# The opening reordered: tile 3's shift in its own buffer, high Wo products ahead of low, rows of products that nobody reads in TensorE's pauses

## The chip, the cores and the metric

The kernel runs on one core of a Trainium2 chip. The metric is the device time of one launch in microseconds (us), and the median of several runs stands for a kernel. A core has five engines that work side by side, each through its own queue in order: TensorE (PE in the profile), VectorE (DVE), ScalarE (ACT), GpSimd (POOL), and SyncE (SP), which here issues the transfers. They meet at semaphores. A page of the profile comes from one profiled execution.

## The reference, cut to what matters

One layer on 2 x 2048 tokens of width 512. `x` is normalised, attends to 64 latent keys per head with the four largest logits, is added and normalised again, and goes through a feed-forward block whose three weight matrices are reduced to three values:

```python
Q = (hidden_states @ Wq.T + bq)...; V = (hidden_states @ Wv.T + bv)...
attn_logits = einsum('bhtd,lhd->bhtl', Q, latent) / sqrt(HD)        # 16 heads, 64 latents
topk_logits, topk_idx = top_k(attn_logits, 4)
weighted = einsum('bhtk,bhtkd->bhtd', softmax(topk_logits), selected)
attn_output = (weighted + V) @ Wo.T + bo

scale = mean(abs(w)) + 1e-8                                          # for W_up, W_gate, W_down
w = clip(round(w / scale), -1, 1) * scale
ffn = (silu(x @ wu.T) * (x @ wg.T)) @ wd.T

x = x + layernorm(attention(layernorm(x)))
x = x + layernorm(ffn(layernorm(x)))
```

## The kernel before

The 4096 tokens are eight chunks of 512, a chunk is four tiles of 128 tokens. Every float32 factor is split into a high and a low float16 half ("hi", "lo"); a product is two or three float16 products that add up in PSUM. The order on each engine is written out by hand, as a list of calls per body. There are five bodies: "first" (attention of chunk 0), "second" (attention of chunk 1 beside the feed-forward block of chunk 0), "mid" in a loop, "last" and "tail". Every body but "first" starts with the Q products of its chunk (`q`), then 16 column blocks of up and gate products (`upgate`), with the attention of the next chunk between them, then the down products.

The change lies in "first" and the head of "second". What happens there in the kernel before:

- **Selection of the four largest**, tile by tile: VectorE finds the maxima (`maxes`) and marks them (`replace`, into `Lr`), POOL subtracts the largest (`shift`, in place in `Lb`), ScalarE takes the exponential (`exps`), VectorE keeps the marked ones (`select`), POOL normalises (`normalise`, line 1242, into `p`), ScalarE and VectorE write the high and low halves (`probs_hi`, `probs_lo`), SyncE transposes both into `PT` (`pt`). `Lb` has two buffers, tile t in buffer t % 2.
- **Value products** (`weigh_half(0)` for tiles 0 and 1, `weigh_half(1)` for 2 and 3), evicted by ScalarE (`vw_half`) with the low half on POOL (`low_a_half`, line 1215).
- **Wo**: `wo_first(0)` gives the output of tiles 0 and 1, the products with the high weights first, then those with the low weights of Wo (from `weights_lo(2)` on VectorE). `wo(2)` and `wo(3)` give the rest. From each output VectorE and POOL make layer norm, residual and second layer norm (`y_a`, `rstd_y`, `y_b`, `rstd_x`, `y_c`), ScalarE and VectorE the rows' two halves (`t2_rows`, `t2_lo`, in `halves[t % 2]`), SyncE the transposed `X1T` (`t2`, line 377).
- **The next chunk's rows** go the same way to `XT` (`ln1_stat(1)`, `s1_rows`, `s1_lo`, `s1`). Their split lies in two buffers in `Lr`, so tile 2 waits for the transposition of tile 0.
- **The three-valued weights**: each matrix is loaded in eight pieces (0 to 7 up, 8 to 15 gate, 16 to 23 down) into memory that is used later for something else; pieces 0 and 8 lie in `X1T`. `abs_sum` adds absolute values per piece, `tern_total(w)` adds those of a matrix, a product with ones (`total`, line 537) adds over the partitions, `tern_scale_of(w)` makes the scale; `round_to(n)` on VectorE (line 1440) rounds a piece, `sign(n)` on ScalarE (line 882) writes the final one. The first transposition of `X1T` waits for signs 0 and 8.

TensorE's order in "first" ends with `wo(3)` and the gate's total, which waits for VectorE. "second" begins with `q(0)`, which waits for all of `XT`. `upgate(0)` and `upgate(1)` run in two halves of 256 tokens, then come the logits of tiles 0 and 1, then `upgate(2)`.

## Time and profile before

| | |
|---|---|
| median of 3 runs | 1037.1 us (1036.57 to 1037.91) |
| the profiled execution | 1038.45 us, its span 1036.7 us |
| mean granted TensorE clock | 0.981 |
| TensorE busy | 968.7 us, 93% of the span |
| VectorE, POOL, ScalarE busy | 731.3, 535.0 and 514.1 us |
| column block 2 of the feed-forward block starts | 121.67 us after the span's start |

The page has the busy share of each engine in 40 equal slices of about 26 us, in tenths. The timeline lists instructions with their start, their duration and, in brackets, the idle time before them with what ended it. All times count from the start of the span, which is 1.75 us shorter than the whole time of the profiled execution.

### The profile page before, as it was taken

What the parts mean: (1) busy time and instruction counts of PE and PEld (TensorE: products, weight loads), DVE (VectorE), ACT (ScalarE), POOL (GpSimd) and SP (SyncE); (2) the same over time, 40 slices, a digit from 0 to 9 for tenths busy, and PEclk for the clock granted to TensorE, in tenths of its full rate; (3) what the DMA queues carried; (4) which work ended last, traced back from release to release, by engine and by line L of the source; (5) the groups of instructions that cost most, each with busy time, mean ns of one, the idle gap of its engine ahead of it and who ended that gap; (6) DMA issues with size and microseconds to landing.
All of it is one profiled execution on the core that took longest, in us unless ns stands there. A gap on an engine that the chain in (4) does not pass through costs nothing.

```text
span 1036.7 us, 17905 instructions
## 1 busy us (share of the span) xinstructions
PE 968.7 (93%) x5738; PEld 470.6 (45%) x5738; DVE 731.3 (71%) x2667; ACT 514.1 (50%) x801; POOL 535.0 (52%) x450
## 2 busy tenths in 40 slices
PE   2736999999999999999999999999999999999997
PEld 1412544445444554445444454445444454445443
DVE  6897799466993789745994768936896669845433
ACT  5777886445445445345444445344553454423430
POOL 2564356664665546564665446664465546642330
PEclk9876999999999999999999999999999999999999
DMA  9943503433123312233013321244022421212001
GB/s 290 401 91 66 164 1 82 102 92 92 22 41 92 83 50 39 55 89 98 12 33 92 74 78 21 41 106 107 10 41 61 91 42 21 41 41 62 1 1 41
DMA packets 149330, 76.91 MB, mean 74 GB/s; under 512 B 135824, under 2 KB 135824, under 8 KB 148112
## 3 DMA queue, kind: packets, MB, share of 16 engines
q1 hardware_dynamic: 149264, 76.18, 29.2%
q8 instruction: 23, 0.38, 0.2%
q14 instruction: 43, 0.35, 0.1%
HBM read 34.21 MB, written 8.39 MB: 41 GB/s over the span
## 4 chain that ended last, share of the span: by engine, by line
PE 60%; DVE 17%; POOL 7%; issue 6%; ACT 6%; DMA 3%; SPq 0%; DVEq 0%; ACTq 0%; POOLq 0%
PE ug L700 34%; PE ug L719 12%; PE ring L546 8%; PE ring L678 3%; DVE Lr L1553 2%; PE ring L594 2%; DMA X1T<-halves 2%; POOL halves L1271 1%; DVE v L1527 1%; DVE halves L1507 1%; DVE row L1642 1%; DMA x_in<-in_x 1%; DVE sty L1645 1%; DVE stx L1665 1%; DVE ugt L1512 1%
## 5 line engine op out<-in xcount | busy, mean ns | idle before, releaser
L1248 POOL TENSOR_TENSOR hT<-ugt,hT 128x512 f16<-128x512 f32 x128 | 166.8, 1303 | 164.9 <-ACT hT L1012 164.9
L700 PE MATMUL ug<-X1T,TU 128*128 128x512 f16 (+1 forms) x1152 | 245.1, 356 | 7.3 <-DVE ugt L1517 4.2
L700 PE MATMUL ug<-X1T,TG 128*128 128x512 f16 (+1 forms) x1152 | 244.8, 355 | 0.0
L719 PE MATMUL ug<-TD,hT 128*128 128x512 f16 x960 | 210.9, 379 | 0.9 <-ACT TD L891 0.9
L999 ACT ACTIVATE ugt<-ug,cu 128x512 f32<-128x512 f32 x128 | 87.9, 687 | 203.0 <-PE ug L700 202.1
L700 PEld LDWEIGHTS ug<-X1T,TU 128*128 128x128 f16 x1152 | 110.0, 98 | 117.5 <-issue 6.0
L700 PEld LDWEIGHTS ug<-X1T,TG 128*128 128x128 f16 x1152 | 112.7, 98 | 108.6
L1512 DVE SCALAR_TENSOR_TENSOR ugt<-ugt,ug 128x512 f32<-128x512 f32 x128 | 87.2, 681 | 99.5 <-ACT ugt L999 98.2
L719 PEld LDWEIGHTS ug<-TD,hT 128*128 128x128 f16 x960 | 93.3, 98 | 115.7 <-issue 3.0
L1553 DVE MATCH_REPLACE8 Lr<-v,Lb 128x68 f32<-128x68 f32 x512 | 102.2, 211 | 0.0
L1517 DVE SCALAR_TENSOR_TENSOR ugt<-ugt,ug 128x512 f32<-128x512 f32 x128 | 87.9, 687 | 4.4
L1584 DVE BATCH_NORM_STATS2 stf<-ug 128x6 f32<-128x512 f32 x30 | 20.8, 694 | 98.3 <-PE ug L719 98.3
L546 PE MATMUL ring<-XT,wq_hi 128*128 128x512 f16 (+1 forms) x288 | 81.4, 370 | 8.8 <-DVE wq_lo L1485 5.8
L1230 POOL TENSOR_TENSOR Lb<-Lb,v 128x1024 f32<-128x1024 f32 x32 | 62.3, 1948 | 41.0 <-DVE Lr L1553 41.0
L1012 ACT ACTIVATE hT<-ugt 128x512 f16<-128x512 f32 x128 | 79.5, 621 | 3.1 <-DVE ugt L1517 3.1
L1527 DVE MAX8 v<-Lb 128x8 f32<-128x64 f32 x512 | 69.0, 208 | 0.4
L546 PE MATMUL ring<-XT,wv_hi 128*128 128x512 f16 x224 | 66.6, 379 | 0.0
L1242 POOL TENSOR_TENSOR p<-Lb,r 128x1024 f32<-128x1024 f32 x24 | 45.6, 1901 | 34.8 <-DVE Lb L1568 34.8
L546 PE MATMUL ring<-XT,wq_lo 128*128 128x512 f16 (+1 forms) x144 | 53.2, 370 | 0.0
L840 ACT ACTIVATE xn<-x,nbx,rsx 128x512 f32<-128x512 f32 x28 | 22.7, 810 | 58.6 <-DVE nbx L1676 38.7
L678 PE MATMUL ring<-wo_hi,qaT_hi 128*128 128x512 f16 x120 | 46.2, 385 | 5.4 <-POOL qaT_lo L1215 3.8
L974 ACT ACTIVATE halves<-p 128x1024 f16<-128x1024 f32 x28 | 29.4, 1048 | 43.5 <-POOL p L1242 38.9
(208 smaller groups left out, 1474.6 us busy)
## 6 DMA issues: line engine op xcount, KB each, us to landing
out_dram<-Lr SPq DMA_DIRECT2D x32, 256.0 KB, 3.1
x_in<-in_x SPq DMA_DIRECT2D x7, 1024.0 KB, 5.3
x<-in_x SPq DMA_DIRECT2D x28, 256.0 KB, 3.4
PT<-in_Wd SPq DMA_DIRECT2D x8, 512.0 KB, 6.5
hT<-in_Wu SPq DMA_DIRECT2D x4, 512.0 KB, 8.4
hT<-in_Wg SPq DMA_DIRECT2D x4, 512.0 KB, 15.5
x_in<-in_Wd SPq DMA_DIRECT2D x4, 512.0 KB, 5.3
x_in<-in_x SPq DMA_DIRECT2D x4, 256.0 KB, 4.2
```

Of the source, the lines that this page charges most:

```text
L546: last = pe.matmul(bank[:, cols], wT[w][a][:, k, m * P:(m + 1) * P], XT[:, b, k, cols], start=(n == 1), stop=(stop and n == 3 * KD), skip_ ...
L678: last = pe.matmul(ring[:, bank, :], qaT[a][:, k, t * P:(t + 1) * P], wT[2][b][:, k, :], start=(n == 1), stop=(n == 3 * KD))
L700: last = pe.matmul(ug[:, 2 * (e % 2) + s, cols], w[:, k, e * P:(e + 1) * P], X1T[:, b, k, cols], start=(k == 0 and b == 0), stop=(k == KD ...
L719: last = pe.matmul(down_bank(kind, t), hT[:, a, e, t * P:(t + 1) * P], td[:, e, :], start=(first and e == of[0] and a == 0), stop=(final a ...
L999: act.activation(ugt[:, e % 2, :], ug[:, 2 * (e % 2), :], ACT.Tanh, scale=cu[:, 0:1]).then_inc(tanh_ready, 1)
L1012: act.activation(hT[:, 0, e, :], ugt[:, 2 + e % 2, :], ACT.Copy).then_inc(h_hi, 1)
L1230: pool.tensor_tensor(buf, buf, v8[:, t % 2, :, 0:1].broadcast_to([P, H, NL]), ALU.subtract).then_inc(shifted, 1)
L1248: pool.tensor_tensor(hT[:, 1, e, :], ugt[:, 2 + e % 2, :], hT[:, 0, e, :], ALU.subtract).then_inc(h_lo, 1)
L1512: dve.scalar_tensor_tensor(out=ugt[:, e % 2, :], in0=ugt[:, e % 2, :], scalar=1.0, in1=ug[:, 2 * (e % 2), :], op0=ALU.add, op1=ALU.mult).t ...
L1517: dve.scalar_tensor_tensor(out=ugt[:, 2 + e % 2, :], in0=ugt[:, e % 2, :], scalar=HS, in1=ug[:, 2 * (e % 2) + 1, :], op0=ALU.mult, op1=ALU ...
L1527: last = dve.max(v8[:, t % 2, h, :], Lb[:, t % 2, h, 0:NL])
L1553: last = dve.match_replace(Lr[:, h, :], v8[:, t % 2, h, :], Lb[:, t % 2, h, :], HIT)
```

## The change

It touches the lists of calls of "first" and the head of "second", and some helpers.

1. Tile 3's shift writes into a buffer of its own in `TU` (`exp_rows`) and waits for the maxima of tile 3 instead of the replacement. Shift 3 stands ahead of normalisation 2, exponential 3 follows exponential 2 directly, normalisation 3 stands ahead of the low halves of the attention rows on POOL, selection 3 ahead of `sums(3)` on VectorE.
2. The next chunk's rows get four split buffers instead of two (two of them in `TU`). On ScalarE tiles 1 to 3 follow each other directly, and four absolute sums stand behind them.
3. `wo_first` is cut in two: the high products, then the value products of tiles 2 and 3 and the total of the up weights, then the low products. `weights_lo(2)` keeps its place but one sum stands ahead of it.
4. `keep_busy(n)` issues n products of 512 columns from `wT[0][0]` into a PSUM bank that nobody reads: 10 ahead of the first value products (behind the low half of tile 1's weights), 10 behind them, 6 behind the high Wo products, 6 behind the low ones.
5. Pieces 0 and 8 are rounded by POOL (`round_to` there), piece 0 behind `rstd_y(2)`, piece 8 behind `rstd_x(0, 2)`.
6. The total of the gate weights (`total(weight_sum(1), ...)`) moves from behind `wo(3)` to behind `q(1)`, into another bank; `q(0)` no longer waits for the gate's scale. On VectorE the total's first step and the scale stand behind `y_a(3)` and `y_b(2)`.
7. On ScalarE `t2_rows(0, 1)` stands ahead of `sign(8)`.

```diff
+        ROUND_POOL = (0, 8)
...
+                half = tu32[:, (2176, 3200)[t - 2]:(2176, 3200)[t - 2] + D] if t >= 2 else out_buf[t]
...
+        def exp_rows(kind, t):
+            if kind == "first" and t == 3:
+                return tu32[:, 2 * D:2 * D + H * NL].rearrange("p (h l) -> p h l", h=H)
...
-                        if kind == "second":
-                            pe.wait_ge(tern_step, 2)
...
+                def keep_busy(n):
+                    for _ in range(n):
+                        pe.matmul(ring[:, 2, :], wT[0][0][:, 0, 0:P], wT[0][0][:, 1, :], start=True, stop=True)
...
+                    wait(pe, l_ready, i, 8, 8)
+                    wait(pe, p_lo, i, TT, 2)
+                    keep_busy(10)
                     weigh_half(0)
+                    keep_busy(10)
                     wo_first(0)
+                    keep_busy(6)
+                    weigh_half(1)
                     wait(pe, l_ready, i, 8, 8)
                     total(weight_sum(0), tot[:, 0:1], tot_ready, 1, tota_ready)
-                    weigh_half(1)
+                    wo_first(1)
+                    keep_busy(6)
                     wo(2)
                     pe.wait_ge(tern_step, 1)
                     wo(3)
-                    wait(pe, y_ready, i, TT, 1)
-                    total(weight_sum(1), tot[:, 1:2], tot_ready, 2, tota_ready)
...
                     for m in range(KD):
                         q(m)
+                        if kind == "second" and m == GATE_TOTAL:
+                            wait(pe, a32_ready, j, KD, KD)
+                            total(weight_sum(1), tot[:, 1:2], tot_ready, 2, tota_ready)
...
+                    if kind == "first" and t == 3:
+                        wait(pool, top8, i, TT, t + 1)
+                    else:
+                        wait(pool, replaced, i, TT, t + 1)
+                    pool.tensor_tensor(exp_rows(kind, t), buf, v8[:, t % 2, :, 0:1].broadcast_to([P, H, NL]), ALU.subtract).then_inc(shifted, 1)
...
+                    pool.wait_ge(w_loaded[n], 16)
+                    pool.wait_ge(tern_scale, w + 1)
+                    pool.tensor_scalar(src, src, iw[:, w:w + 1], MAGIC, ALU.mult, ALU.add).then_inc(pool_rounded, 1)
```

POOL's queue from normalisation 2 of chunk 0 on, in the kernel before (`Lb<-Lb,v` is a shift, `p<-Lb,r4p` a normalisation, `qaT_lo` the low halves of the attention rows, `rs`, `rsy` and `rsx` roots of the layer norms, `Lr<-Lb,Lr` a low half of the next chunk's rows):

```order
L1242 TENSOR_TENSOR p<-Lb,r4p 128x1024
L1230 TENSOR_TENSOR Lb<-Lb,v 128x16x64
L1215 TENSOR_TENSOR qaT_lo<-x_kept,qaT_hi 128x256 x4
L1239 TENSOR_SCALAR r4p<-r 128x16
L1242 TENSOR_TENSOR p<-Lb,r4p 128x1024
L1184 TENSOR_TENSOR rs<-va,nh 128x4
L1184 TENSOR_TENSOR rsy<-vay,nh 128x1 x2
L1271 TENSOR_TENSOR Lr<-Lb,Lr 128x512
L1215 TENSOR_TENSOR qaT_lo<-x_kept,qaT_hi 128x256 x4
```

And with the change, with what each waits for (`TU<-Lb,v8` is shift 3):

```order
L1258 TENSOR_TENSOR TU<-Lb,v8 128x1024 [waits top8]
L1267 TENSOR_SCALAR r4p<-r4 128x16 [waits p_lo,recip_ready]
L1270 TENSOR_TENSOR p32<-Lb,r4p 128x1024 [waits p_raw,recip_scaled]
L1267 TENSOR_SCALAR r4p<-r4 128x16 [waits p_lo,recip_ready]
L1270 TENSOR_TENSOR p32<-TU,r4p 128x1024 [waits p_raw,recip_scaled]
L1240 TENSOR_TENSOR qaT_lo<-x1_kept,qaT_hi 128x256 [waits va_hi] x4
L1209 TENSOR_TENSOR rs1<-va1,nh 128x4 [waits ln1_var]
L1307 TENSOR_TENSOR Lr<-Lb,Lr 128x512 [waits x_hi]
L1240 TENSOR_TENSOR qaT_lo<-x1_kept,qaT_hi 128x256 [waits a_hi] x4
```

Shift 3 went ahead of normalisation 2 and the four low halves went behind normalisation 3. Further down the same queue, the change has the two roundings between the roots:

```order
L1209 TENSOR_TENSOR rsy<-vay,nh 128x1 [waits y_var]
L1280 TENSOR_SCALAR X1T<-X1T,iw 128x1024 [waits tern_scale,w_loaded0]
L1209 TENSOR_TENSOR rsy<-vay,nh 128x1 [waits y_var]
L1209 TENSOR_TENSOR rsx<-vax,nh 128x1 [waits ln2_var]
L1280 TENSOR_SCALAR X1T<-X1T,iw 128x1024 [waits tern_scale,w_loaded8]
L1209 TENSOR_TENSOR rsx<-vax,nh 128x1 [waits ln2_var]
```

Both rows of line 1280 are new on this engine; before, VectorE did them. ScalarE's queue around signs 0 and 8 before (`xn<-x` and `halves<-xn` are the two steps of a tile's second-norm rows, `TU<-X1T` sign 0, `TG<-X1T` sign 8, `p<-ring` and `qaT_hi<-p` the eviction of a Q product):

```order
L874 ACTIVATE xn,asum<-hT 128x1024
L882 ACTIVATE TU<-X1T,nmagic 128x4x256
L840 ACTIVATE xn<-x,nbx,rsx 128x512
L852 ACTIVATE halves<-xn 128x512
L882 ACTIVATE TG<-X1T,nmagic 128x4x256
L840 ACTIVATE xn<-x,nbx,rsx 128x512
L852 ACTIVATE halves<-xn 128x512
L840 ACTIVATE xn<-x,nbx,rsx 128x512
L852 ACTIVATE halves<-xn 128x512
L927 ACTIVATE p<-ring,bqs 128x512
```

And with the change:

```order
L895 ACTIVATE xn,asum<-hT 128x1024 x2
L906 ACTIVATE TU<-X1T,nmagic 128x4x256
L861 ACTIVATE xn<-x,nbx,rsx 128x512
L873 ACTIVATE halves<-xn 128x512
L861 ACTIVATE xn<-x,nbx,rsx 128x512
L873 ACTIVATE halves<-xn 128x512
L906 ACTIVATE TG<-X1T,nmagic 128x4x256
L861 ACTIVATE xn<-x,nbx,rsx 128x512
L873 ACTIVATE halves<-xn 128x512
L951 ACTIVATE p<-ring,bqs 128x512
```

Sign 8 stands one tile later, directly ahead of tile 2's rows.

## Rows read from the trace of the kernel before

**Rows 1.** The page's 40 slices: TensorE's busy tenths.

```profile
PE   2736999999999999999999999999999999999997
```

**Rows 2.** Timeline of TensorE: start, duration, engine, line, operation, tiles, count.

```profile
64.62 0.63 PE L623 MATMUL ug<-PT,latV_hi 64*32 64x256 f16 x16 [10.00 <-DMA PT<-row]
...
65.64 0.46 PE L623 MATMUL ug<-PT,latV_lo 64*32 64x256 f16 x8
68.37 0.59 PE L658 MATMUL ring<-wo_hi,qaT_hi 128*128 128x512 f16 x1 [2.27 <-POOL qaT_lo L1215]
...
78.54 2.46 PE L658 MATMUL ring<-wo_lo,qaT_hi 128*128 128x512 f16 x8 [4.09 <-DVE wo_lo L1485]
...
99.55 1.01 PE L546 MATMUL ring<-XT,wq_hi 128*128 128x512 f16 x2 [2.95 <-DMA XT<-Lr]
...
106.73 0.59 PE L546 MATMUL ring<-XT,wq_hi 128*128 128x512 f16 x2
...
111.91 1.04 PE L700 MATMUL ug<-X1T,TU 128*128 128x256 f16 x8
...
121.67 1.90 PE L700 MATMUL ug<-X1T,TU 128*128 128x512 f16 x8
```

**Rows 3.** The chain of waits: start, duration, what the chain ran through.

```profile
111.37 5.12 DMA X1T<-halves
116.63 3.65 PE ug L700 x32
```

**Rows 4.** Timeline of ScalarE.

```profile
98.22 1.13 ACT L882 ACTIVATE TG<-X1T,nmagic 128x1024 f16<-128x1024 f32 x1
...
106.26 0.63 ACT L852 ACTIVATE halves<-xn 128x512 f16<-128x512 f32 x1
...
109.41 0.63 ACT L852 ACTIVATE halves<-xn 128x512 f16<-128x512 f32 x1
...
118.58 0.69 ACT L999 ACTIVATE ugt<-ug,cu 128x512 f32<-128x512 f32 x1
```

**Rows 5.** Timeline of POOL.

```profile
64.68 1.93 POOL L1230 TENSOR_TENSOR Lb<-Lb,v 128x1024 f32<-128x1024 f32 x1 [1.50 <-DVE Lr L1553]
...
71.51 1.90 POOL L1242 TENSOR_TENSOR p<-Lb,r4p 128x1024 f32<-128x1024 f32 x1
...
91.16 0.55 POOL L1184 TENSOR_TENSOR rsx<-vax,nh 128x1 f32<-128x1 f32 x1 [0.21 <-DVE vax L1670]
92.20 1.16 POOL L1271 TENSOR_TENSOR Lr<-Lb,Lr 128x512 f16<-128x512 f32 x1 [0.49 <-ACT Lr L826]
```

**Rows 6.** Timeline of VectorE.

```profile
58.80 1.16 DVE L1575 TENSOR_TENSOR row<-p,row 128x1024 f16<-128x1024 f32 x1
...
65.48 2.21 DVE L1575 TENSOR_TENSOR halves<-p,halves 128x1024 f16<-128x1024 f32 x1
...
79.61 0.75 DVE L1642 SCALAR_TENSOR_TENSOR row<-ring,clo,bo_b 128x512 f32<-128x512 f32 x1 [1.06 <-PE ring L658]
...
84.54 1.21 DVE L1415 TENSOR_REDUCE asum<-hT 128x1 f32<-128x1024 f32 x1
...
90.93 0.15 DVE L1670 TENSOR_SCALAR vax<-mvx 128x1 f32<-128x1 f32 x1
...
97.03 0.75 DVE L1440 TENSOR_SCALAR X1T<-X1T,iw 128x1024 f32<-128x1024 f32 x1
```

**Rows 7.** Stretches of TensorE: length, busy, matmuls, granted clock, DMA share, GB/s.

```profile
72.00:74.00 2.00, 2.00 (x8) 0.77 0.00 0
...
76.00:78.00 2.00, 0.00 (x0) 1.00 0.48 94
...
80.00:82.00 2.00, 2.00 (x45) 0.50 0.00 0
```

**Rows 8.** The tile XT, its four transpositions of 85.8 to 96.3: time to landing.

```profile
DMA to landing us min/median/max: 3.0/3.0/3.0
```

**Rows 9.** Timeline of SyncE.

```profile
100.44 12.16 SPq L377 DMA_TRANSPOSE X1T<-halves  x4
```

139 lines of the change are left out of this document (77 added, 62 removed).

## The prediction

> **What bounds the kernel now.** I read the page first, its busy digits: in TensorE's row the first four of 40 slices stand below 9 tenths, and all behind them but the last at 9 or more [rows 1]. So the kernel is an opening, bound by chains across all engines, and a long body bound by TensorE. The change touches the opening alone: its worth is how much earlier or later the body starts. The marker is the start of column block 2 of the up and gate products, 121.67 us [rows 2]. Behind it TensorE hardly pauses, and where it does it waits for VectorE's gating, whose inputs shift with the opening. So I carry a shift of this marker to the end undiminished.
>
> The chain that ended last shows what sets the marker: the transfer of X1T's last tile lands 5.12 us after 111.37, and the products start at 116.63 [rows 3]. Behind it stands the chain of tiles 2 and 3 on ScalarE and VectorE, and behind that the Wo products of those tiles. The Q products (99.55 on) end at 111.9, just as late [rows 2]. ScalarE is the third: its first tanh is at 118.58, after four signs [rows 4].
>
> **Shift 3 ahead of two normalisations.** Today shift 3 waits for the replacement and runs 64.68 to 66.6 [rows 5]. In its own buffer it needs only tile 3's maxima, done near 58.5, and runs at 58.6 to 60.5. What it meets there: VectorE's low half of tile 1's weights, read at 58.80 with 1.16 us. A VectorE operation of this kind that met this very shift took 2.21 us, ending 1.1 us after the shift's end [rows 5, 6]. So the half ends at 61.6, not 59.96; its transposition and the first value products move from 64.62 to about 66.2, 1.6 us later [rows 2]. Selection 2 moves too, so normalisation 2 ends at 65.0, not 63.2. Tile 3 gains: its selection comes straight behind its replacement, at 66.4, and normalisation 3 starts at 69.5 instead of 71.51 [rows 5]: 2.0 us earlier.
>
> But on POOL normalisation 3 now stands ahead of the low halves of the attention rows. The first of these ends at 72.0; today TensorE gets it at 68.37 [rows 2]. The fourth ends at 75.1, since ScalarE's third and fourth rows stand behind high half 3.
>
> **First output tile.** From 75.1, ten high products remain at the full clock, where 24 products take 5.18 us (106.73 to 111.91), 0.216 each [rows 2]. Then 6 unread products, the value products of half 1 (1.5, as from 64.62 to 66.10), the total of two short products, and four of eight low products. At the full clock that is 75.1 + 2.2 + 1.3 + 1.5 + 0.9 + 0.3 for the total and the hand-over = 81.3. At the half clock the sixteen high products take 6.8 us from 72.1, and tile 0 is out at about 83.6. Today it is 79.61 [rows 6]. So +1.7 to +4.0. Which clock? Today it rises at 73, survives a pause of 4.1 us that ends at 78.54, and is half again at 80 [rows 2, 7]. The new stretch has 10 unread products from 61.8, 10 more until 69.6, a pause of 2.5 us, then high products that come in four pieces until 75.1. That is thin, and I take 82.8, nearer the half clock: +3.2.
>
> **Next chunk's rows to the Q products.** The last LN2 variance of tile 1 stands at 91.08 today [rows 6], 11.5 us behind the first output. Out of this stretch go one rounding (0.75) and two sums (1.21 each) [rows 6]: 3.2 us, 8.3 are left, 91.0 or 91.1. On POOL the root (0.55) and the last low half of the next chunk's rows (1.15) follow, since rstd_x 1 stands ahead of it; transposition 3.0 with 0.3 of hand-over [rows 5, 8]. The Q products start at 96.0 (94.5 to 96.8), not 99.55: 3.5 us **earlier**. This is the gain of the change. The unread products cost nothing there: those in front of the second half's output lie in waits for POOL.
>
> **The gate total behind two Q products.** Today the gate's scale is there at 97.03, when VectorE rounds piece 8 [rows 6]. Now the total stands behind Q 0 and Q 1, which take 7.2 us from 99.55 to 106.73, partly at the half clock [rows 2]; total and scale add 0.6. 96.0 + 7.2 + 0.6 = 103.8, 6.8 us **later**. Queued behind the scale on VectorE: low half 1, the bias of tile 2, and all of tile 3's row. The rounding itself is now POOL's. No row shows a POOL operation of 1024 columns with one input. VectorE's takes 0.75 [rows 6]; POOL's with two inputs takes 1.90 [rows 5]. I take 1.4, on POOL's side because it is POOL's engine, with both ends kept. Sign 8 adds 1.13 [rows 4]: 103.8 + 0.1 + 1.4 + 1.2 = 106.5, where today it ends at 99.35. (The Trainium skill, GPSIMD Engine Reference, section 3.1, gives 1.03 cycles an element where a port binds: an estimate of 0.9 us with its 1.2 GHz, by which the sum would be 0.5 us less; no run here shows it yet.)
>
> **What waits for sign 8.** SyncE's transpositions of X1T wait for both first signs, because X1T's memory holds pieces 0 and 8. Today they start at 100.44, and the sign is no matter [rows 9]. Now the first starts at 106.6 and lands at 109.6. ScalarE's copy of tile 2 reuses the buffer of tile 0 and waits for it: 109.6, read at 106.26 today [rows 4]. From there: copy 0.54, Q 0 evicted 1.24, tile 3's row 1.4, its low half 0.8: 113.6, and its transposition is issued at 113.75 instead of 111.37 [rows 3]. It lands after 5.1: block 0's second half starts at 118.9, +2.3.
>
> ScalarE: tile 3's copy is followed by tanh 0 after 9.17 us (109.41 to 118.58) [rows 4]. New copy at 112.25, tanh at 121.4. The gating takes 2.1 more, so block 2 can start at 123.6, not 121.67: **+1.9**.
>
> **Sum.** I also placed all instructions of both orders from 48 us on one after another, each with its row's duration, started when its engine was free and its waits were met. For the old order this gives tanh 0 at 117.4, 1.1 us early; it leaves out small delays between engines. For the new order against the old it gives +2.7 to +5.2 at the marker, by where the clock's changes fall and by the rounding. The hand chain gives +1.9 because it uses some of today's intervals, delays in them, on one side only. I take +2.8. The profiled execution took 1038.45 us (span 1036.7); it would be 1041.25. It lies 1.35 above the median of the runs, 1037.1, so I predict **1039.9**. Ends: with the full clock and a rounding of 0.75 tile 0 is out at 81.3, the copy of tile 2 is at 107.4, tanh at 119.2, block 2 at 121.7: 0.0. With half clock and 1.90: +5.2.
>
> **Rival 1: no change (1037.1 to 1039.0).** The unread products keep the clock full from about 66 us on, and POOL's rounding is short; then the earlier Q products (5 us) pay for the later scale, and the marker moves by 0 to +1.9, say 1038.1. For it: the clock outlived 4.1 us of pause [rows 2, 7], the new pauses up to 78 us are shorter. Against it: it was half again after 1.2 us of work, so little work does not hold it. (The Trainium skill, TensorE: Matmul & The Clock Gate, Part 1, says the slow clock is the default and activity releases it. By that rule this rival is the design working: the sum would be near 0. The trace agrees that work raises the clock; whether so few products hold it, no row shows.)
>
> **Rival 2: faster (about 1034.8).** If the first output comes no later than now, POOL's row chain gives Q at 93, Q 0 and Q 1 run at the full clock (24 products, 5.2 us), and sign 8 ends by 101: then X1T's first tile lands at 104.2, before ScalarE's copy of tile 2 at 106.26 would want it, and everything moves by 2 to 2.5 us. Place: Q start. Point from which it decides: sign 8 before 103. For it: the next chunk's rows no longer stand behind ScalarE's sums. Against it: POOL and VectorE would have to pass each other at 58.6, where the rows show that they don't [rows 5, 6].
>
> **Rival 3: the unread products are in the way (1042).** Each group of ten takes 4.3 us at the half clock; the one that starts at 61.8 ends at 66.1, with nothing to spare before the transposition lands, and the two groups of six then delay the second value products and tile 2. Worth +4 to +5.
>
> **Chances.** Forecast and rival 3 (over +2.1 us) 0.60, rival 1 0.27, rival 2 0.13. A measurement of this kernel tells about 0.2% (2.1 us) from no change; so faster 0.13, same 0.27, slower 0.60. The range leaves out most of rival 2 and a tail beyond the upper bound: 1035.8 to 1042.6.
>
> **What would show it.** Low half of tile 1's weights at 2.2 us or more wide, with shift 3 beside it; first value products near 66; first output near 82.8; Q products near 96, ahead of today; gate total near 103.5; sign 8 ending near 106.5, the transpositions of X1T starting right behind it; ScalarE's copy of tile 2 idle for the landing of tile 0; tanh 0 past 120. Wrong would make it: a clock at 1.00 from 66 to 90, a first output before 80.5, or sign 8 before 103.

## The result and the profile after

The changed kernel takes 1038.56 us (median of 17 runs, 1037.07 to 1041.59), the kernel before 1037.17 us (17 runs, 1035.59 to 1038.06). The ratio is 1.0020, 95% interval 1.0013 to 1.0027: slower by 1.4 us by the medians, by 2.1 us by the ratio and by 1.3 to 2.8 us by its interval. The prediction was 1039.9 us, slower by 2.8: the sign is right, and the size lies at the upper end of that interval. The measured 1038.56 us also lies in the range that rival 1 gave for "no change" (1037.1 to 1039.0), so the time alone does not choose between the two; the trace does, below.

The page of the changed kernel, its busy tenths of TensorE, to be read beside [rows 1]:

```profile
PE   2767799999999999999999999999999999999997
```

The body is as full as before. In the opening the third slice (52 to 78 us) went from 3 tenths to 6, part of it unread products, and the fourth from 6 to 7. The fifth (104 to 130 us) fell from 9 to 7: there new waits have appeared.

TensorE's timeline of the changed kernel (start, duration, engine, line, operation, tiles, count, idle time before it):

```profile
60.62 4.14 PE L658 MATMUL ring<-wq_hi 128*128 128x512 f16 x10 [5.74 <-DVE row L1622]
...
65.94 2.33 PE L658 MATMUL ring<-wq_hi 128*128 128x512 f16 x10
...
93.48 1.01 PE L560 MATMUL ring<-XT,wq_hi 128*128 128x512 f16 x2 [6.22 <-DMA XT<-TU]
...
101.10 0.28 PE L551 MATMUL ug<-tot,ones 128*128 128x1 f32 x2
...
109.41 1.87 PE L715 MATMUL ug<-X1T,TU 128*128 128x256 f16 x8 [2.82 <-DMA X1T<-halves]
...
115.68 1.03 PE L715 MATMUL ug<-X1T,TU 128*128 128x256 f16 x8 [1.31 <-DMA X1T<-halves]
...
121.93 1.89 PE L715 MATMUL ug<-X1T,TU 128*128 128x512 f16 x8 [1.15 <-DVE ugt L1562]
```

Against [rows 2]: the Q products start at 93.48 instead of 99.55, 6 us earlier, the total of the gate stands behind two of them at 101.10, and TensorE then waits for X1T at 109.41 and at 115.68. Column block 2 starts at 121.93, where it was 121.67.

VectorE's timeline, against [rows 6]:

```profile
57.70 2.77 DVE L1622 TENSOR_TENSOR row<-p,row 128x1024 f16<-128x1024 f32 x1
...
79.97 0.75 DVE L1689 SCALAR_TENSOR_TENSOR row<-ring,clo,bo_b 128x512 f32<-128x512 f32 x1 [0.26 <-PE ring L673]
...
101.42 0.16 DVE L1465 TENSOR_SCALAR sw<-ug 128x1 f32<-128x1 f32 x1 [3.28 <-PE ug L551]
```

GpSimd's (POOL), against [rows 5]:

```profile
57.46 1.93 POOL L1258 TENSOR_TENSOR TU<-Lb,v 128x1024 f32<-128x1024 f32 x1 [0.23 <-DVE v L1572]
...
101.95 1.53 POOL L1280 TENSOR_SCALAR X1T<-X1T,iw 128x1024 f32<-128x1024 f32 x1 [3.19 <-DVE iw L1469]
```

ScalarE's, against [rows 4]:

```profile
103.52 1.15 ACT L906 ACTIVATE TG<-X1T,nmagic 128x1024 f16<-128x1024 f32 x1 [5.73 <-POOL X1T L1280]
...
108.04 0.63 ACT L873 ACTIVATE halves<-xn 128x512 f16<-128x512 f32 x1 [2.67 <-DMA X1T<-halves]
...
119.68 0.67 ACT L1023 ACTIVATE ugt<-ug,cu 128x512 f32<-128x512 f32 x1
```

And the chain of waits of the changed kernel in this stretch (start, duration, what it ran through):

```profile
90.25 3.10 DMA XT<-TU
93.35 0.14 issue
93.48 7.78 PE ring L560 x24
101.27 0.13 PE ug L551 x2
...
101.42 0.17 DVE sw L1465
...
101.61 0.17 DVE iw L1469
...
101.95 1.55 POOL X1T L1280
...
103.52 1.16 ACT TG L906
104.70 3.26 DMA X1T<-halves
```

This is the whole finding in one view: 24 matmuls of two Q products, then a matmul of one column, a scale, a rounding, a sign, and only then the transpositions of the next rows. SyncE's first transposition into X1T is at 104.70; it was at 100.44 [rows 9].

**How to compare executions.** In the profiled execution of the changed kernel everything was already 1.1 us early at 57 us: VectorE's low half of tile 1's weights starts at 57.70, in the kernel before at 58.80 [rows 6]. This start lies between 56.55 and 58.80 us in the fourteen profiled executions, and in either order it differs by over 1 us between executions. So I measure from the start of this operation ("common start" below). From there to the start of column block 2 are 62.87 us before (121.67 - 58.80) and 64.23 after (121.93 - 57.70): the change costs 1.36 us there. Behind block 2 the span still has 1036.7 - 121.67 = 915.03 us before and 1037.3 - 121.93 = 915.37 after, so the shift is carried to the end nearly undiminished, as the prediction said. A second mark is the first output tile, VectorE's first row from the output of Wo (79.61 before, 79.97 after): 20.81 and 22.27 us from the common start.

### The profile page after: what moved, and what is told of

The parts are those of the page before. It is cut to its first block, busy times and chain, and to the rows that moved or that the text cites. A ratio compares the mean times of both kernels' runs of the same rounds, so it can differ in the third digit from the quotient of the medians.

```text
span 1037.3 us, 17973 instructions
## 1 busy us (share of the span) xinstructions
PE 976.0 (94%) x5770; PEld 472.9 (46%) x5770; DVE 729.9 (70%) x2665; ACT 513.9 (50%) x801; POOL 535.3 (52%) x452
## 4 chain that ended last, share of the span: by engine, by line
PE 60%; DVE 16%; ACT 7%; POOL 6%; issue 6%; DMA 3%; SPq 0%; DVEq 0%; ACTq 0%; POOLq 0%
PE ug L715 34%; PE ug L734 12%; PE ring L560 9%; PE ring L693 3%; DVE Lr L1598 2%; PE ring L606 2%; DMA X1T<-halves 1%; POOL halves L1307 1%; DVE v L1572 1%; DMA x_in<-in_x 1%; DVE halves L1552 1%; DVE row L1689 1%; DVE stx L1712 1%; DVE ugt L1557 1%; DVE sty L1692 1%
## 5 line engine op out<-in xcount | busy, mean ns | idle before, releaser
L1209 POOL TENSOR_TENSOR rsf<-vaf,nh 128x1 f32<-128x1 f32 x32 | 19.7, 616 | 55.8 <-DVE vaf L1636 55.8
```

## The experiments

My theory after the trace, T: the place of the gate total sets the end, through scale, rounding of piece 8, sign 8 and the transpositions that wait for it. Rivals: the unread products or the clock; the collision of shift 3 on GpSimd with VectorE; the rounding on GpSimd.

All runs in one table. "Block 2" is the start of column block 2 from the common start; "first transposition" that of X1T from the common start; the column behind it is from there to ScalarE's first tanh. "First output" counts from the common start too, and the last column is block 2 less the first output. All are from each run's timelines, so from one execution each.

| run | median us | ratio to before (95%) | block 2 | first transposition | to tanh | first output | block 2 behind it |
|---|---|---|---|---|---|---|---|
| before | 1037.17 | | 62.87 | 41.64 | 18.14 | 20.81 | 42.06 |
| changed | 1038.56 | 1.0020 (1.0013 to 1.0027) | 64.23 | 47.00 | 14.98 | 22.27 | 41.96 |
| e1 total ahead of Q | 1035.69 | 0.9991 (0.9982 to 1.0000) | 62.58 | 44.94 | 14.94 | 23.58 | 39.00 |
| e2 no unread products | 1038.69 | 1.0016 (1.0007 to 1.0025) | 64.07 | 46.87 | 14.95 | 22.02 | 42.05 |
| e3 total, scale, rounding ahead | 1034.82 | 0.9979 (0.9970 to 0.9988) | 59.76 | 42.48 | 15.02 | 23.53 | 36.23 |
| e4 VectorE rounds | 1037.31 | 1.0006 (0.9997 to 1.0015) | 63.65 | 46.04 | 14.90 | 22.25 | 41.40 |
| e5 total behind first Q | 1036.36 | 0.9998 (0.9989 to 1.0007) | 62.31 | 44.70 | 14.90 | 23.35 | 38.96 |
| e6 before, total late | 1047.36 | 1.0103 (1.0087 to 1.0118) | 73.88 | 53.53 | 18.10 | 21.51 | 52.37 |
| e7 before, unread products | 1037.26 | 1.0007 (0.9998 to 1.0016) | 63.20 | 42.83 | 18.12 | 22.17 | 41.03 |
| e8 shift 3 later | 1039.97 | 1.0033 (1.0021 to 1.0045) | 66.28 | 49.09 | 14.94 | 23.98 | 42.30 |
| e9 clock kept for Q | 1036.36 | 0.9993 (0.9984 to 1.0002) | 63.59 | 46.40 | 14.93 | 24.16 | 39.43 |
| e10 e3 and sign 8 earlier | 1031.40 | 0.9944 (0.9930 to 0.9958) | 57.22 | 39.04 | 15.92 | 22.24 | 34.98 |
| e11 e3 and clock kept | 1032.44 | 0.9957 (0.9944 to 0.9971) | 58.55 | 41.39 | 14.91 | 22.43 | 36.12 |
| e12 e10 and clock kept | 1032.53 | 0.9952 (0.9938 to 0.9965) | 58.29 | 39.93 | 16.10 | 23.34 | 34.95 |

Two readings of it carry the rest. Block 2 against the kernel before and the ratio of the run move together within 1 us in all but one (e6: +11.01 and +10.7 us; e10: -5.65 and -5.8). The one is e9, +0.72 and -0.7: its profiled execution, span 1036.2 us, is the slowest of its eleven. And in the changed kernel's order the time from the first transposition of X1T to the first tanh is 14.9 to 15.0 us, wherever the transposition stands, but for e10 and e12, where sign 8 stands earlier; in the order of before it is 18.1.

The last column is a check on both. The first output comes at 22.0 to 24.2 us in the changed kernel's order, and it differs between executions whose order up to there is the same. Behind it the runs sort themselves more cleanly: against the changed kernel e1 and e5 are 3.0 us earlier, e9 2.5, e3 5.7, e10 and e12 7.0; e11 is 0.1 us ahead of e3, and e8 is 0.3 us later.

### e1: the gate total ahead of the Q products

```diff
                 if att:
+                    if kind == "second":
+                        wait(pe, a32_ready, j, KD, KD)
+                        total(weight_sum(1), tot[:, 1:2], tot_ready, 2, tota_ready)
                     for m in range(KD):
                         q(m)
-                        if kind == "second" and m == GATE_TOTAL:
-                            wait(pe, a32_ready, j, KD, KD)
-                            total(weight_sum(1), tot[:, 1:2], tot_ready, 2, tota_ready)
```

> The changed kernel with the one-column gate total put ahead of the Q products of the next chunk instead of behind the second of them; nothing else differs. In the changed kernel the total ran at 101.10 us, the scale at 101.42, GpSimd's rounding of piece 8 at 101.95 (1.53) and the sign of piece 8 at 103.52. Theory T (the chain total, scale, rounding, sign 8, transposes of the next chunk's rows sets the end): the total then runs as soon as VectorE's last absolute sum is there (about 93 us), the scale follows its place on VectorE, behind the low half of t2 (about 96.5), the rounding ends by 98.5 and sign 8 starts near 99.5 at its place in ScalarE's order; block 2 of the up and gate products starts 2.5 to 4 us before the changed kernel's 121.93, and the whole run is 1.5 to 3.5 us faster than the changed kernel, so at or below the kernel before (1034.8 to 1036.8 against 1037.2). Rival U (the unread products and the clock set the end): the end moves by less than 0.5 us, since the Q products stand where they stood. Rival S (shift 3's collision on the shared path of VectorE and GpSimd sets it): less than 0.5 us as well.

Measured: 1035.69 us, ratio 0.9991, its interval clear of the changed kernel's; by the ratios 3.0 us faster than the changed kernel. Block 2 starts at 119.42. The total and the scale in its timelines of TensorE and VectorE:

```profile
93.77 0.56 PE L551 MATMUL ug<-tot,ones 128*128 128x1 f32 x2 [6.04 <-DVE tot L1460]
```

```profile
98.51 0.15 DVE L1465 TENSOR_SCALAR sw<-ug 128x1 f32<-128x1 f32 x1
```

The one-column total costs TensorE 0.4 us (the Q products start at 94.18) in a pause that is 6.04 us long. The scale comes 4.2 us later, since on VectorE it stands behind the low half of a tile's rows and the layer norm of tile 2: there is a second queue to leave. Theory T holds; U and S, which wanted less than 0.5 us, fall.

### e2: the changed kernel without unread products

```diff
                     wait(pe, p_lo, i, TT, 2)
-                    keep_busy(10)
                     weigh_half(0)
-                    keep_busy(10)
                     wo_first(0)
-                    keep_busy(6)
                     weigh_half(1)
...
                     wo_first(1)
-                    keep_busy(6)
                     wo(2)
```

> The changed kernel without any of its 32 unread products (groups of 10, 10, 6 and 6); the order of all else is the same. Theory T: they are not what lost the time; without them the granted clock of TensorE between 64 and 80 us is half for longer, the first output tile comes 0.5 to 2 us later than 79.97, and what the chain behind the gate total gives is nearly the same: within 1.5 us of the changed kernel either way. Rival U (the unread products stand in the way): block 2 of the up and gate products starts 1 to 3 us before 121.93, the run is 1 to 3 us faster than the changed kernel. Rival K (they hold the clock and are the part of the change that gains): 1.5 to 3 us slower than the changed kernel, 1040 to 1041.5.

Measured: 1038.69 us, ratio 1.0016; no difference from the changed kernel. They do hold the clock. In the view of stretches (length, busy time of TensorE, its weight loads, VectorE, ScalarE and GpSimd, then the granted clock, the DMA share and GB/s) the granted clock is the third number from the end. Without them:

```profile
66.00:68.00 2.00, 0.88 (x39) 0.38 (x16) 1.97 (x4) 1.64 (x5) 0.00 (x0) 0.50 0.00 0
```

With them (the changed kernel):

```profile
66.00:68.00 2.00, 2.00 (x12) 0.83 (x10) 1.97 (x5) 1.94 (x5) 0.00 (x0) 1.00 0.00 0
...
72.00:74.00 2.00, 1.70 (x5) 0.30 (x4) 1.88 (x3) 1.97 (x5) 1.52 (x2) 0.50 0.00 0
74.00:76.00 2.00, 2.00 (x9) 0.86 (x8) 1.94 (x9) 1.82 (x4) 1.05 (x1) 0.86 1.11 210
```

But when the products that matter come, from 71 us on, the clock is at half in both (0.50 in 72 to 74), and in both it rises in 74 to 76 us (0.80 and 0.86). The first output tile is out 22.27 us from the common start with them, 22.02 without. So this part of the change neither gains nor costs; rivals U and K fall here.

### e3: total, scale and rounding ahead

```diff
                 if att:
+                    if kind == "second":
+                        wait(pe, a32_ready, j, KD, KD)
+                        total(weight_sum(1), tot[:, 1:2], tot_ready, 2, tota_ready)
                     for m in range(KD):
                         q(m)
-                        if kind == "second" and m == GATE_TOTAL:
...
                     rstd_y(3)
-                    rstd_x(0, 2)
                     round_to(8)
+                    rstd_x(0, 2)
...
                     tern_total(1)
+                    tern_scale_of(1)
                     t2_lo(0, 0)
                     y_b(2)
-                    tern_scale_of(1)
```

> The changed kernel with three moves: the gate total ahead of the Q products, the scale of the second gate directly behind VectorE's sum for that total (ahead of the low half of t2), and GpSimd's rounding of piece 8 ahead of a one-column operation that waited in front of it. Theory T: scale near 93.5 to 95 us instead of 101.42, rounding of piece 8 done by 97, sign 8 near 98; the copies of halves for the next chunk's rows then wait only for their transposes; block 2 of the up and gate products at 116.5 to 119 instead of 121.93 and the run 3 to 5 us faster than the changed kernel (1033.5 to 1035.5), faster than both kernels. Rival U or S: within 1 us of the changed kernel, as the pieces behind then wait for TensorE's Q products or for the transfers all the same.

Measured: 1034.82 us, ratio 0.9979: 4.3 us faster than the changed kernel by the ratios and faster than both. GpSimd's rounding:

```profile
95.56 1.12 POOL L1280 TENSOR_SCALAR X1T<-X1T,iw 128x1024 f32<-128x1024 f32 x1 [0.74 <-DVE iw L1469]
```

It ends at 96.68, and sign 8 still starts only at 98.90: ScalarE has its copy of tile 1 in front. SyncE starts the transpositions at 100.05. The mark moved by 4.5 us from the common start, the transposition by the same 4.5.

### e4: piece 8 rounded by VectorE

```diff
-        ROUND_POOL = (0, 8)
+        ROUND_POOL = (0,)
...
                     rstd_x(0, 2)
-                    round_to(8)
                     rstd_x(0, 3)
...
                     tern_scale_of(1)
+                    round_to(8)
                     t2_lo(0, 1)
```

> The changed kernel with piece 8 rounded by VectorE (as the kernel before did) directly behind the scale of the second gate, instead of by GpSimd; GpSimd keeps the rounding of piece 0. Theory T: the rounding costs about 0.64 us on VectorE where GpSimd took 1.53 behind a hand-over, so sign 8 starts 0.7 to 1.1 us earlier than 103.52 and block 2 of the up and gate products 0.5 to 1.1 us earlier; the run is 0.4 to 1.1 us faster than the changed kernel. Rival (the GpSimd rounding is hidden and the delay is elsewhere): within 0.3 us. Rival (VectorE's own order behind it is what binds): 0.3 to 0.8 us slower.

Measured: 1037.31 us; sign 8 at 102.47 (changed: 103.52), block 2 0.58 us earlier from the common start. By the ratios 1.5 us faster, but the two intervals overlap at their edge (1.0013 to 1.0015). The direction and the 1 us at sign 8 agree with T: GpSimd's rounding is a small part of the chain, not hidden.

### e5: the gate total behind the first Q product

```diff
-        GATE_TOTAL = 1
+        GATE_TOTAL = 0
```

> The changed kernel with the gate total behind the first Q product of the next chunk instead of the second (eight groups, 3.8 us at the half clock, instead of sixteen, 7.6 us). Theory T with VectorE's order as the next limit: the total runs near 97.3, and the scale, which stands behind a blocked normalisation of x on VectorE, at 98.3 to 98.8 as in the run with the total ahead of all Q products (98.51); sign 8 near 100.6, block 2 of the up and gate products near 119.4 to 120, the run 2.3 to 3 us faster than the changed kernel: one Q product of delay costs nothing, the second costs all of it. Rival (each Q product ahead of the total costs in proportion): half of the gain, 1.4 us. Rival (the place of the total is not the cause, but the writes to another bank): no gain.

Measured: 1036.36 us; total at 98.17, scale at 98.76, sign 8 at 100.85, block 2 at 119.64, 62.31 from the common start where e1 has 62.58. The trace agrees with a free first Q product: VectorE comes to the scale at about 98.5 anyway. By the run times it gives 2.3 us of e1's 3.0, and their intervals overlap. The proportional rival (1.4 us) is not excluded by the run times alone; block 2 speaks against it, since from the common start it is 1.9 us earlier than in the changed kernel, in e1 1.7 us.

### e6: the kernel before, its total late

```diff
-            return (ring[:, 3, 0:1], ring[:, 0, 0:1], ring[:, plans["second"][("S", 0, 0)][0], 0:1])[w]
+            return (ring[:, 3, 0:1], ug[:, 3, 0:1], ring[:, plans["second"][("S", 0, 0)][0], 0:1])[w]
...
-                        if kind == "second":
-                            pe.wait_ge(tern_step, 2)
...
                     wo(3)
-                    wait(pe, y_ready, i, TT, 1)
-                    total(weight_sum(1), tot[:, 1:2], tot_ready, 2, tota_ready)
                     return
...
                         q(m)
+                        if kind == "second" and m == 1:
+                            wait(pe, a32_ready, j, KD, KD)
+                            total(weight_sum(1), tot[:, 1:2], tot_ready, 2, tota_ready)
```

> The kernel before with one edit: its gate total, which ran at 96.25 us in the 6 us in which TensorE waited for rows, is put behind the second Q product of the next chunk. Theory T: the Q products start at 99.55, at the half clock for about 4 us, so the total runs near 105.5 to 106, the scale near 106 instead of 96.64, sign 8 near 107.5 instead of 98.22, and the transposes of the next chunk's rows (100.44 before) at 108.5 or later; block 2 of the up and gate products 4 to 8 us after 121.67, the run 4 to 8 us slower (1041 to 1045). It is more than in the changed kernel since the Q products start later here. Rival (TensorE's clock or the other parts set the changed kernel's loss): less than 1 us.

Measured: 1047.36 us, ratio 1.0103: 10.7 us slower, more than I had expected. TensorE's timeline and ScalarE's:

```profile
98.99 1.01 PE L546 MATMUL ring<-XT,wq_hi 128*128 128x512 f16 x2 [5.07 <-DMA XT<-Lr]
...
107.09 0.28 PE L537 MATMUL ug<-tot,ones 128*128 128x1 f32 x2
```

```profile
108.58 1.15 ACT L881 ACTIVATE TG<-X1T,nmagic 128x1024 f16<-128x1024 f32 x1 [10.70 <-DVE X1T L1439]
```

Sign 8 is 11.5 us later from the common start (50.90 against 39.42), as T says, but my range for the end was 4 to 8: I had the transpositions start at 108.5 or later, and SyncE starts them at 111.21. The total itself is a part of it, at 107.09 where I had 105.5 to 106: the two Q products took 8.1 us. The rest I left out is what stands behind the scale in VectorE's queue: the rounding, the row of tile 2's output and its statistics, and only then the low half of tile 0's rows, for which the first transposition waits. In [rows 6] and [rows 9] that is 97.03 to 100.44, 3.4 us, and I had counted the sign alone. In the changed kernel the same place of the total costs only 3 us. Its Q products start 5.5 us earlier, and the rows of tiles 2 and 3's outputs stand ahead of the scale there; that these two make the difference is read from the orders, no run takes them apart.

### e7: the kernel before with unread products

```diff
                         v(m)
+                    wait(pe, l_ready, i, 8, 8)
+                    wait(pe, p_lo, i, TT, 2)
+                    keep_busy(10)
                     weigh_half(0)
+                    keep_busy(10)
                     wo_first(0)
+                    keep_busy(6)
                     wait(pe, l_ready, i, 8, 8)
```

> The kernel before with three of the changed kernel's groups of unread products (10, 10 and 6) ahead of the first value products, ahead of Wo's first products and ahead of the second value products. Theory T and the run without unread products (which left the changed kernel where it was): within 0.7 us of the kernel before, either way; the granted clock of 66 to 72 us is full instead of half, and what TensorE gains there it waits again for VectorE's and GpSimd's pieces. Rival K (a fuller clock there brings the first output tile and the end earlier): 1 to 2 us faster. Rival U (they are in the way): 1 to 2 us slower.

Measured: 1037.26 us, ratio 1.0007 (0.9998 to 1.0016), block 2 0.33 us later: no difference, as in e2. The same part judged in both kernels gives the same answer. In this one execution the first output came 1.36 us later than before (22.17 against 20.81): the granted clock was 0.50 in 78 to 80 us, when the eight low Wo products ran, and they took 3.60 us, 2.46 before [rows 2]. In e6, which has no unread products, the same eight took 3.44 us, so such a difference comes without them too.

### e8: shift 3 back behind normalisation 2

```diff
                     shift(2)
-                    shift(3)
                     normalise(2)
+                    shift(3)
                     normalise(3)
```

> The changed kernel with shift 3 behind the normalisation of tile 2 on GpSimd, where the kernel before had it, and still in its own buffer. In the changed kernel it ran at 57.46 beside VectorE's two-operand operations, of which one took 2.77 us instead of 1.16 and pushed the normalisation of tile 2 to 61.80. Theory T: the gain of the collision gone (VectorE 1.1 to 1.6 us earlier, normalisation 2 at 59.5 to 60.5) is given back by shift 3's later place and by tile 3's attention weights, so the end moves little: within 1 us of the changed kernel, a little slower likelier than faster. Rival S (the collision is what the change lost): 1 to 2 us faster than the changed kernel, the first output tile near 78.5.

Measured: 1039.97 us; block 2 2.05 us later from the common start, by the ratios 1.4 us slower than the changed kernel (the intervals overlap). The collision is gone, in its timeline of VectorE:

```profile
56.84 1.16 DVE L1622 TENSOR_TENSOR row<-p,row 128x1024 f16<-128x1024 f32 x1
```

and of GpSimd:

```profile
59.33 1.90 POOL L1270 TENSOR_TENSOR p<-Lb,r4p 128x1024 f32<-128x1024 f32 x1
61.19 1.93 POOL L1258 TENSOR_TENSOR TU<-Lb,v 128x1024 f32<-128x1024 f32 x1
```

VectorE's operation takes 1.16 us instead of 2.77, and the normalisation of tile 2 starts 2.49 us behind the common start instead of 4.10. Still tile 3's normalisation starts 11.62 us behind the common start instead of 10.74 (68.46 - 56.84 and 68.44 - 57.70), so the early shift brings it forward by 0.88 us in spite of the collision. The first output tile is out at 23.98 instead of 22.27, but the other 0.8 us of that is the clock, which in e8 came back to its full level only 19.4 us behind the common start, in the changed kernel after 16.8; behind the first output block 2 is just 0.3 us later. So the early shift is worth about 0.9 us, not the 2.05 of block 2, and the run times, with intervals that overlap, do not show it clear of noise. Rival S, which had this run 1 to 2 us faster, falls.

### e9: the clock kept for the Q products

```diff
-                def keep_busy(n):
+                def keep_busy(n, bank=ring[:, 2, :]):
...
-                        pe.matmul(ring[:, 2, :], wT[0][0][:, 0, 0:P], wT[0][0][:, 1, :], start=True, stop=True)
+                        pe.matmul(bank, wT[0][0][:, 0, 0:P], wT[0][0][:, 1, :], start=True, stop=True)
...
                     wo(3)
+                    keep_busy(26, ug[:, 2, :])
                     return
```

> The changed kernel, its gate total still behind the second Q product, with 26 more unread products (into a bank that nothing uses then) in the pause between Wo's last product and the first Q product. In the run with only the total moved that pause was 6.0 us long and the granted clock fell to 0.50 in it; the 24 matmuls of the first two Q products then took 7.62 us in the changed kernel. Theory T, refined: the price of the total's place is the time of those two Q products, and more than 2 us of it is the half clock. With the clock full they take 5.2 to 5.3 us (24 by 0.217), the total runs at 98.7 to 99.0 if the products end before 93.5, the scale at 99.0 to 99.3 instead of 101.42, block 2 of the up and gate products 1.5 to 2.5 us before 121.93 and the run 1 to 2.5 us faster than the changed kernel. Rival U (unread products get in the way, or the clock doesn't set this place): within 0.5 us, or slower by what they end behind 93.5.

Measured: 1036.36 us, ratio 0.9993, its interval clear of the changed kernel's; 2.8 us faster by the ratios. TensorE's timeline:

```profile
95.28 0.59 PE L560 MATMUL ring<-XT,wq_hi 128*128 128x512 f16 x2 [0.56 <-DMA XT<-TU]
...
100.46 0.28 PE L551 MATMUL ug<-tot,ones 128*128 128x1 f32 x2
```

The two Q products take 5.18 us instead of 7.62, with the granted clock at 1.00 through all of 88 to 108 us. Stretches of the changed kernel for comparison: 0.50 in 94 to 96, 0.88 in 98 to 100:

```profile
94.00:96.00 2.00, 2.00 (x7) 0.60 (x6) 0.47 (x1) 1.47 (x3) 0.00 (x0) 0.50 0.00 0
...
98.00:100.00 2.00, 2.00 (x9) 0.83 (x8) 0.14 (x1) 0.00 (x0) 0.55 (x1) 0.88 0.00 0
```

So 2.4 us of the price of the total's place is the half clock. Unread products do gain, where they stand in a pause directly ahead of the products that a chain waits for. The profiled execution shows less of it than the run times do (block 2 0.64 us earlier): its first output was 1.9 us later than the changed kernel's, for a reason ahead of the edit that I take up below; counted from the first output, block 2 is 2.5 us earlier, near the 2.8 of the run times.

### e10: sign 8 ahead of tile 1's copies, on e3

```diff
                     t2_rows(0, 0)
-                    t2_rows(0, 1)
                     sign(8)
+                    t2_rows(0, 1)
```

> The kernel with total, scale and rounding moved ahead (the run at 1034.82 us), with ScalarE's sign of piece 8 between the copies of tile 0 and of tile 1 instead of behind tile 1's. There GpSimd's rounding ended at 96.68 while sign 8 ran at 98.90 and SyncE sent the first transpose of the next chunk's rows at 100.05; ScalarE had 0.89 us of wait at 96.63. Theory T: sign 8 at 96.8 to 97.1, first transpose at 98.0 to 98.4; but TensorE's Q products ended there at 108.17 without a wait behind them, so they are the next bound, and of the 2 us only the second half of block 0 and ScalarE's copies gain: block 2 of the up and gate products 0 to 1 us before 117.33, the run within 0.8 us of it. Rival (the transposes alone set the end): 1.5 to 2 us faster.

Measured: 1031.40 us (5 runs, 1030.81 to 1031.68), ratio 0.9944: 3.6 us faster than e3, 5.8 us faster than the kernel before and the fastest of all. ScalarE, SyncE and TensorE:

```profile
95.49 1.15 ACT L906 ACTIVATE TG<-X1T,nmagic 128x1024 f16<-128x1024 f32 x1
```

```profile
96.66 9.98 SPq L391 DMA_TRANSPOSE X1T<-halves  x4
```

```profile
114.84 1.89 PE L715 MATMUL ug<-X1T,TU 128*128 128x512 f16 x8
```

I had expected at most 0.8 us, because TensorE went from the Q products into block 0 without a wait in e3. That was the wrong engine: block 2 waits for the gating behind ScalarE's first tanh, and ScalarE, with its copies of tiles 2 and 3 freed from the transpositions, came to it 2.5 us earlier. The rival, in which the transpositions set the end, was nearer with 1.5 to 2 us. Part of it is chance: the first output was 1.3 us earlier in this execution than in e3's. So the 3.6 us of the run times are more than this mechanism accounts for: 2.5 us at block 2, and 1.3 us with the first output's share taken off. ScalarE's two waits for a landed transposition in e3 (1.85 and 0.45 us) have become waits for VectorE's second layer norm of tiles 2 and 3 (1.43 and 0.45 us), which is the next bound.

### e11 and e12: the clock kept, on e3 and on e10

e11 is e3 with the edit of e9, e12 is e10 with it:

```diff
                     wo(3)
+                    keep_busy(26, ug[:, 2, :])
                     return
```

> The kernel with total, scale and rounding moved ahead (1034.82 us), with 26 unread products in the pause ahead of the gate total and the Q products. Theory T: the Q products, which ran there from 94.86 to 108.17 with the clock at half until about 101, take 10.4 us and end near 105.3; block 0 of the up and gate products then waits for the transposes instead (the first two landed near 105.2), so it starts near 105.3 to 106, and block 2 up to 1 us before 117.33, since ScalarE's signs and tanh behind its Q copies come next; the run 0 to 1.5 us faster (1033.3 to 1034.8). Rival U: 0.5 us or more slower.

> Both of the last two edits on the kernel with total, scale and rounding moved ahead: sign 8 ahead of tile 1's copies, and 26 unread products ahead of the total. Theory T: the two bounds (transposes of the next chunk's rows, Q products) both move by 2 us or more, so the gain is more than the sum of the two alone: block 2 of the up and gate products 1.5 to 2.5 us before 117.33, the run 1 to 2.5 us faster than 1034.82 (1032.3 to 1033.8), the fastest of all. Rival (the end is by now set by ScalarE's own queue of copies and signs): less than 0.5 us better than the better of the two alone.

Measured: 1032.44 and 1032.53 us. On e3 it gives 2.3 us by the ratios (the intervals touch), more than expected; on e10 nothing, where I had expected 1 to 2.5. The traces do not show a gain in either: block 2 of e11 is 1.2 us earlier than e3's, but so is its first output by 1.1, and behind the first output e11 differs from e3 by 0.1 us and e12 from e10 by nothing. In both e3 and e11 ScalarE waits for the same landing of a transposition (1.85 and 1.88 us), and in both the first transposition starts 18.95 us behind the first output, whatever the Q products' clock. So where the 2.3 us come from stays open; chance in five runs is not excluded. In e12 TensorE is through with the Q products early and waits again for X1T (1.13 us), and the time from the first transposition to the tanh is 16.10 us: ScalarE first waits 1.60 us for VectorE's second layer norm of tile 2 and then runs its own queue with two waits of about 0.5 us. That queue, and the layer norm in front of it, set the end.

## Why the prediction came out as it did

**What bounds, and the marker: right.** Between column block 2 and the end lie 914.5 to 916.3 us in all fourteen executions.

**Shift 3 ahead of two normalisations: right, in kind and in size.** The forecast had VectorE's low half at 2.8 us from its start (58.80 to 61.6); it is 2.77. It had normalisation 3 at 10.7 us from the common start (69.5 - 58.8); it is 10.74. What this step left open, whether the move pays at all, e8 answers for that normalisation: 0.88 us.

**First output tile: the step that was mis-sized.** Forecast 24.0 us from the common start (82.8 - 58.8), measured 22.27. The term was the clock: I took the half clock nearly through, and it was half only for about 71 to 74.5 us. (The half-clock end of the term, 83.6, is not a full sum either: behind 72.1 + 6.8 it leaves 4.7 us for what takes 4.0 at the full clock, when the products in it at the half clock make it about 6.) In ten executions of the changed kernel's order with shift 3 early, this number falls in two groups: 22.02 to 22.43 (changed, e2, e4, e10, e11) and 23.34 to 24.16 (e1, e3, e5, e9, e12). Between them nothing differs in the code up to there but, in e2, the unread products. In e1 the granted clock is still 0.50 in 74 to 76 us and 0.91 in 76 to 78, in the changed kernel it is 0.86 in 74 to 76. So the same order has its first output up to 1.9 us earlier or later in one execution or another, and my range of 81.3 to 83.6 (22.5 to 24.8) caught one group and just missed the other. Of the three signs that I had named as proof of error one came, by the trace's own times: a first output before 80.5 (79.97). From the common start it did not come (22.27, where 80.5 would be 21.7). The other two did not: the granted clock was 0.50 in 72 to 74 us, and sign 8 started at 103.52.

**Next chunk's rows to the Q products: right in time, wrong in what it is worth.** Forecast 37.2 us from the common start, measured 35.78; behind the first output it is 13.2 against 13.51. But the step calls the earlier Q products "the gain of the change", and no trace shows the end waiting for them; what the change gained stands elsewhere, below.

**The gate total behind two Q products: right, and this is the cause.** Forecast 7.2 us for the two, measured 7.62; the rounding on GpSimd was taken as 1.4 and is 1.53. Scale forecast at 103.8, measured 101.42; from the start of the Q products that is 7.8 and 7.94. (The Trainium skill's GPSIMD Engine Reference, section 3.1, gives 1.03 cycles an element, which with its 1.2 GHz makes an estimate of 0.9 us; the runs show 1.12 at best, and the measurement decides.) e1 and e6 show it from both sides: taken away it gives 3 us, put into the kernel before it costs 10.7. This is also what decides against rival 1: there the unread products were to keep the clock full from about 66 us on, and it was 0.50 in 72 to 74 us with them; that its range held the result is no sign for its mechanism. Rival 3 falls with e2, and rival 2 had the Q products at 93, which came (93.48), but sign 8 by 101, which did not.

**What waits for sign 8: right to 0.2 us.** From the first transposition to tanh the forecast had 14.8 us (106.6 to 121.4), measured 14.98; ScalarE's copy waits 2.67 us for the landing, as the step said. In it one term was wrong and had no effect: the last tile's transposition landed after about 3.1 us here, not 5.1. The chain of waits at the end runs through ScalarE's queue, not through that landing.

**Sum: where 1 us was lost.** By hand the chain gave +1.9 at block 2, measured +1.36. Part of that agreement is luck. Against the trace the chain had the first output 1.7 us too late and the way from there to the first transposition 0.9 us too short (23.8 us against 24.73), and the two errors partly cancel. I then raised it to +2.8 by a placement of all instructions that gave 2.7 to 5.2. Its working is not on show, so which of its terms was too large stays open; by its own words its range hung on the clock and on the rounding. The hand chain alone, 1038.45 + 1.9 - 1.35 = 1039.0, would have been within 0.5 us of the median. The lesson of that step: I trusted the fuller method over the one whose terms were rows.

**Where the gain went.** The change loses 5.4 us up to the first transposition (41.64 to 47.00), and it gains 3.2 us from there to tanh (18.14 to 14.98). ScalarE's timeline of the kernel before shows what the 3.2 us were:

```profile
105.41 0.81 ACT L840 ACTIVATE xn<-x,nbx,rsx 128x512 f32<-128x512 f32 x1 [3.55 <-DVE nbx L1676]
```

Its copy of tile 2 waited 3.55 us for VectorE's second layer norm of that tile, which stood behind the scale of the gate and the rows of the outputs of tiles 2 and 3. With the change these rows stand ahead of the scale (item 6 of the change), and the copy waits 2.67 us for the landing of the first transposition instead. The Q products come 5.0 us earlier from the common start, but ScalarE waits for none of them in either kernel, and in e9 and e11 a full clock for them leaves this way at 14.9 us. The last 0.84 us of the sum, 5.36 - 3.16 - 0.84 = 1.36, are from tanh to block 2 (3.09 to 2.25), and they are not the change's: e6 and e7, in the order of before, have 2.25 too. In the profiled execution of the kernel before TensorE came late to block 2, behind a transposition that took 5.12 us to land [rows 3]. Up to tanh the change costs 2.2 us, near the 2.1 of the ratio. With the loss taken away (e3, e10) the gain is there.

**What stays open.** Why one of the four transpositions of X1T lands after 5.1 us in the kernel before and in e2, after 5.0 in e7, 4.7 in e3 and 4.3 in e6, and none after more than 3.3 in the others: no run isolates it. Why the clock's rise falls in two groups is open too; and that the wider spread of the changed kernel's times (1037.07 to 1041.59) comes from it is argued, not shown.

## What to carry to other kernels

A tiny instruction on an in-order engine (here one column, 0.3 us) comes as late as what stands in front of it in its queue, and here its result held up work on three other engines: when a long operation is brought forward past it, look at who waits for the small one, and put it into the pause ahead instead. Judge a bundle of edits part by part, since this one held a gain of some 3 us and a loss of some 5 at two places of one chain, and only their difference showed. Before a difference at the end is put down to an edit, take off what varies between executions of the same order (here the first output, by up to 2 us). And after one bound is lifted, look for the next in the queue of the engine that the end waits for, not in the engine that happens to be busy.

## What the runs showed of the hardware

- **A two-operand operation of VectorE waits out one of GpSimd.** The same VectorE operation on 128 x 1024 takes 1.16 us alone (e8) and 2.77 us where GpSimd's shift of 1.93 us runs from 0.24 us before it: it ends 1.08 us behind the shift, so nearly all of it was done behind the shift. The 2.21 us on which the forecast rested [rows 6] are the same thing met later: that operation, too, ends 1.08 us behind the end of its shift (65.48 + 2.21 against 64.68 + 1.93).
- **GpSimd with one input** takes 1.12 us on 128 x 1024 (e3, with VectorE waiting beside it) and 1.53 us with VectorE at a two-operand operation (changed kernel), which itself took 1.48 us there and 0.74 in e3. VectorE's takes 0.75 [rows 6].
- **The granted clock falls in a pause and is paid for later.** It is 1.00 in 88 to 90 us in e3 (last product at 88.4), 0.50 from 92 us on, and with TensorE busy without a gap from 94.4 us it is 0.50 in 98 to 100 and 0.78 in 100 to 102. In the changed kernel, whose Q products start at 93.48, it is 0.88 in 98 to 100. (The Trainium skill, TensorE: Matmul & The Clock Gate, Part 1, says that the moment of the rise varies from run to run, by half a microsecond either way; the traces agree that it varies, but by more: behind the common start the first Wo products reach the full clock after 16.8 us in the changed kernel and after 19.4 in e1.)
